# Routed FFN around attention on one core: experts packed eight to a register word, the next tile's rows transposed behind h, and the first steps in another order

## Chip, cores and metric

One Trainium2 chip, one of its cores. The metric is the device time of one execution in microseconds, lower is better. The kernel before took 728.1 us, the median of three runs (727.32 to 729.77).

## What is computed

The input x has 16 x 256 = 4096 rows of 128 numbers (fp32). Three residual stages follow each other:

```python
x = x + 0.5 * ffn(layernorm(x))      # pass 1
x = x + attention(layernorm(x), context)   # 8 heads of 128, 512 keys
x = x + 0.5 * ffn(layernorm(x))      # pass 2, same weights

def ffn(x):      # 8 experts, D 128, F 512; each row goes to the one with the largest logit
    top = argmax(x @ gate_w.T + gate_b + expert_bias)
    for e in range(8):
        h = relu(x @ w1[e] + b1[e])
        out += (top == e) * (h @ w2[e] + b2[e])
```

## The kernel before

**Routing and tiles.** T = 32 tiles of 128 rows. Rows are sorted by expert, so that each tile has one expert, in SLOTS = 39 slots (each expert's region is rounded up to whole tiles: 32 + 8 - 1). In pass 1 VectorE computes for all rows where they go, GpSimd gathers each slot's rows by an indirect DMA (12 buffers), and SyncE stores the results packed. In pass 2 the rows are scattered into sorted regions while attention goes on; SyncE loads the slots, and GpSimd scatters the results to the output. Which expert a slot has is known only on the chip: a table `expert_of_tile` (ET, 39 numbers). In pass 2 it comes in two parts: 17 early slots (EARLY), and 22 late ones, whose table needs the last rows of attention.

**One pass.** Every engine has its own instruction stream, written out as a loop over steps m with lags, and waits for the others by semaphores. In step m TensorE does, in this order (`experts`, L1609):

1. y of tile m-4 (L1649 to L1653): 4 matmuls of 256 columns, 4 of 128, one for the bias; into bank 6 or 7;
2. the transpose of tile m's normed rows (L1659), into bank 0 or 1;
3. h of tile m-1 (L1674, and `three` at L1599 to L1601): 16 matmuls of 128 columns, in fp16 planes (hi by hi, hi by lo, lo by hi).

ScalarE does in step m hT_hi of tile m-2 (L848), xT_hi of tile m (L853) and slot_xn, the normed rows, of tile m+1 (L838). VectorE does the two y additions of tile m-5 (L1330, L1333), hT_lo of tile m-2 (L1338) and xT_lo of tile m (L1342). y waits for hT_lo, for the additions two tiles earlier (its bank) and for the weight planes; h waits for xT_lo, hT_lo four tiles earlier and its planes.

**The expert's registers.** The weights' address depends on the slot's expert. TensorE's stream loads experts into registers with one instruction for up to BATCH = 13 slots (`experts_of`, L387 to L395, the load is L394): ahead of h of slots 0, 13, 17 and 30, in both passes. In pass 2 the one for slot 17 stands behind a wait for the late table. From such a register, register operations make the addresses: the program has groups of three (multiply or add, multiply, add) as one fused operation, and single additions. These, waits and loads are executed by TensorE's sequencer; they aren't counted as busy.

**What else the first steps hold.** Pass 1 begins while other work is still going on, and each engine's stream has a fixed place for it, by step:

```python
W1_PLANES = {0: [3], 1: [4], 2: [5], 3: [6], 4: [7]}           # VectorE: w1_hi, w1_lo of expert e (L1214, L1216)
W2_HIGHS = {1: [2], 3: [3], 4: [4], 5: [5], 6: [6], 7: [7]}    # ScalarE: w2 high plane (L771)
W2_LOWS = {5: [3], 6: [4], 7: [5], 8: [6], 9: [7]}             # VectorE: w2 low plane (L1221)
```

Planes 0 to 2 of w1 are made before step 0 by VectorE, w2's high planes 0 and 1 in step 0 by ScalarE, and w2's low planes 0 to 2 by GpSimd behind its gathers (L617, L621). Tile j of the first eight waits for plane pair j of w1 and w2, whichever expert it has. `head(6)` and `head(7)` are the evacuations on ScalarE (L719, L714) of the last two heads' attention products, which TensorE makes in steps 0 and 1. `packed_rows` (L1108 to L1113) is the table by which SyncE stores packed results, `b2_scale` (L1210) scales a bias that y needs, `scales` (L1233 to L1248) computes the attention's power-of-two scales in step 8, from squares that ScalarE makes in steps 2 and 3 (L736). From step 9 on, ScalarE makes a high plane of the attention matrices every second step (L727, L729; `split_at`), VectorE or GpSimd the low one a step later.

**Around tile 12 of pass 2.** The first 12 slots are loaded ahead. SyncE then fills the tails of the eight regions (`fill_tails`, L402), when the last counts are known in VectorE's step 7, and only then loads slot 12 (L507).

Of the kernel before, what the change touches and what calls it, by code (L numbers as in the profile page):

```python
# [4 lines left out]
P = 128  # L5
# [3 lines left out]
def macaron_kernel(nc, x, context, Wq, Wk, Wv, Wout, bout, gate_w, gate_b, expert_bias, w1, b1, w2, b2, out):  # L9
# [31 lines left out]
    SLOTS = T + E - 1  # L41
# [9 lines left out]
    BATCH = 13  # L51
# [14 lines left out]
    with ctx:  # L66
# [51 lines left out]
        ET = sb("expert_of_tile", [P, SLOTS], i32)  # L118
# [145 lines left out]
        routed = sem("routed")  # L264
# [34 lines left out]
        BATCHES = [*range(0, EARLY, BATCH), *range(EARLY, SLOTS, BATCH)]  # L299
# [15 lines left out]
        SCALES_AT, NORMS = 8, 3 * P  # L315
# [8 lines left out]
        EMPTY_LINKS, EARLY_LINKS = 12, 13  # L324
# [60 lines left out]
        def expert(eng, j):  # L385
            return register_of(eng, ET[0:1, j:j + 1], E - 1)
# [24 lines left out]
        SPLIT_STEP, BIAS_AT = 9, 4  # L411
# [4 lines left out]
        W1_PLANES = {0: [3], 1: [4], 2: [5], 3: [6], 4: [7]}  # L416
        W2_HIGHS = {1: [2], 3: [3], 4: [4], 5: [5], 6: [6], 7: [7]}
# [111 lines left out]
        def _(pool):  # L529
# [25 lines left out]
            def consts_of_second_routing():  # L555
# [3 lines left out]
                          allow_small_or_imprecise_dtypes=True)  # L559
                pool.iota(TIDX[:, :], pattern=[[1, SLOTS]], base=0, channel_multiplier=0,  # L560
# [128 lines left out]
        def _(act):  # L689
# [143 lines left out]
            def experts(r):  # L833
# [8 lines left out]
                def step(m):  # L842
# [36 lines left out]
                if r == 0:  # L879
                    w2_high(0)  # L880
# [53 lines left out]
        def _(dve):  # L934
# [116 lines left out]

            def experts_of_tiles():
                step, count = table_step[0], table_count[0]
# [3 lines left out]
                v.tensor_scalar(ET[:, :], ETF[:, :], float(E - 1), None, ALU.min).then_inc(routed, 1)  # L1057
# [59 lines left out]
            def blocks(first, n, i, after_):  # L1117
                step, count = table_step[1], table_count[1]
                own = slice(first, first + n)
                sel = SEL[:, 0:n, :]  # L1120
# [5 lines left out]
                elif i == 2:  # L1126
                    link(v.tensor_scalar(ET[:, own], ETF[:, 0:n], float(E - 1), None, ALU.min), step, count)
# [138 lines left out]
            pick_rows(1)  # L1266
            split_ranks(0)
# [13 lines left out]
            w1_planes(1)  # L1281
            b1_scale()
            w1_planes(2)
# [39 lines left out]
            def experts(r):  # L1323

                def step(m):
# [27 lines left out]
                    if r == 0 and m == 0:  # L1353
                        packed_rows()
# [183 lines left out]
        def _(pe):  # L1538
# [70 lines left out]
            def experts(r):  # L1609
                loaded = {}  # L1610

                def step(m):
# [17 lines left out]
                    if live(m, 1) and m - 1 in BATCHES:  # L1630
                        some = slice(m - 1, min([b for b in BATCHES if b > m - 1] + [SLOTS]))
                        loaded.update(zip(range(some.start, some.stop), experts_of(pe, some)))
                    if live(m, 4):
# [20 lines left out]
                        last.then_inc(s_y, 1)  # L1654
                    if r == 1 and m > STAT_STEP:
                        last_group(m)
                    if live(m, 0):
                        pe.wait_ge(s_xn, SLOTS * r + m + 1)
                        pe.transpose(BK[m % 2][:, 0:P], XSN[:, m % 2, :], IDN[:, :]).then_inc(s_xT, 1)  # L1659
                    if live(m, 1):  # L1660
                        j = m - 1
                        e1 = loaded[j]
# [296 lines left out]
```

## Time and profile before

| | |
|---|---|
| runs | 727.32, 728.1, 729.77 us |
| profiled execution | 726.75 us, of it 725.0 us from first to last instruction |
| mean granted TensorE clock | 0.979 |
| busy: TensorE, its weight loads | 93%, 63% |
| busy: VectorE, ScalarE, GpSimd | 82%, 80%, 47% |
| pass 1, attention, pass 2 | about 49 to 144, 144 to 614, 614 to 713 us |

The page counts an engine as busy only for its own instructions; TensorE's 93% therefore has in it neither waits nor register work. A matmul's duration in a row is its time through the array, and neighbours overlap: their starts tell the pace. Times in rows are microseconds from the first instruction. "[1.08 <-DVE ...]" is the idle time of the engine just before and what seems to have ended it, "issue" where nothing that the profile shows did. PEld is TensorE's weight load, PEldq its sequencer.

### The profile page before, as it was taken

To read this page: it belongs to the slowest core of one execution; us is meant where nothing else is said; L and a number is where in the kernel's file an instruction comes from. 1 tells how busy PE (TensorE), PEld (TensorE's weight loads), DVE (VectorE), ACT (ScalarE), POOL (GpSimd) and SP (SyncE) were. 2 spreads that over 40 slices of the span, in tenths; PEclk is the share of its full clock that TensorE was granted. 3 is DMA by queue.
4 is the path that set the end of the run, shared out by engine and by line. 5 is a ranking of instruction groups with operands and counts; after the bars stand their busy time and mean duration, and the time that the engine had idled before them with its cause. 6 is when DMAs were issued, how large, how long until landed. Compare 5 with 4: busy or idle time off the path is not lost.

```text
span 725.0 us, 16959 instructions
## 1 busy us (share of the span) xinstructions
PE 675.6 (93%) x5175; PEld 458.5 (63%) x5175; DVE 592.5 (82%) x1598; ACT 578.7 (80%) x1407; POOL 341.0 (47%) x437
## 2 busy tenths in 40 slices
PE   8798888989999999999999999999999999988982
PEld 7677767845666655655655655565565665776872
DVE  6799867887888888888888888888889888676762
ACT  4688666789999999989989989999998997645650
POOL 7056466534434346346445434534634644354433
PEclk9899999999999999999999999999999999999997
DMA  9911333120000000000000000000000020032210
GB/s 244 340 31 33 74 87 82 47 69 2 1 0 1 2 1 16 2 1 11 6 1 9 9 1 5 13 0 1 17 1 2 12 50 0 21 106 54 62 41 5
DMA packets 31029, 26.41 MB, mean 36 GB/s; under 512 B 5001, under 2 KB 26159, under 8 KB 30944
## 3 DMA queue, kind: packets, MB, share of 16 engines
q1 hardware_dynamic: 26496, 18.67, 9.3%
q0 software_dynamic: 3520, 6.40, 3.3%
q8 instruction: 46, 0.75, 0.5%
q10 hardware_dynamic: 928, 0.27, 0.2%
q14 instruction: 39, 0.32, 0.2%
HBM read 15.78 MB, written 10.47 MB: 36 GB/s over the span
## 4 chain that ended last, share of the span: by engine, by line
PE 69%; DVE 14%; ACT 5%; issue 4%; SPq 3%; POOL 2%; DMA 1%; POOLq 0%; DVEq 0%; ACTq 0%
PE bank L1599 14%; PE bank L1601 14%; PE bank L1600 13%; PE bank L1857 13%; PE bank L1649 5%; DVE neg_max L1484 3%; DVE probsT_lo L1490 3%; PE bank L1650 2%; PE bank L1674 2%; DVE hT_lo L1338 2%; ACT probs L894 1%; SPq L448 1%; ACT probsT_hi L901 1%; PE bank L1659 1%; POOL rows L641 1%
## 5 line engine op out<-in xcount | busy, mean ns | idle before, releaser
L657 POOL TENSOR_SCALAR probs<-probs,row_inv 128x512 f32<-128x512 f32 x256 | 177.2, 693 | 250.7 <-DVE row_inv L1495 249.0
L1490 DVE TENSOR_TENSOR probsT_lo<-bank,probsT_hi 128x512 f16<-128x512 f32 x256 | 176.4, 689 | 38.0 <-ACT probsT_hi L901 34.4
L894 ACT ACTIVATE probs<-bank,neg_max_unscaled,unscale_bits 128x512 f32<-128x512 f32 x256 | 199.0, 777 | 8.5
L1484 DVE TENSOR_REDUCE neg_max<-bank 128x1 f32<-128x512 f32 x256 | 175.3, 685 | 24.0 <-PE bank L1601 19.1
L1857 PEld LDWEIGHTS bank<-ident,probs 128*128 128x128 f32 x1024 | 123.8, 141 | 68.5 <-issue 28.8
L1857 PE MATMUL bank<-ident,probs 128*128 128x128 f32 x1024 | 155.0, 274 | 7.4 <-DVE probsT_lo L1490 7.2
L901 ACT ACTIVATE probsT_hi<-bank 128x512 f16<-128x512 f32 x256 | 149.8, 586 | 1.7 <-PE bank L1857 1.7
L889 ACT ACTIVATE neg_max_unscaled<-neg_max,unscale_bits 128x1 f32<-128x1 f32 x256 | 75.1, 293 | 32.2 <-DVE neg_max L1484 27.6
L1599 PE MATMUL bank<-m_hi,xT_hi 128*128 128x512 f16 x256 | 97.0, 379 | 0.8 <-POOL vw_lo L609 0.6
L1601 PE MATMUL bank<-probsT_hi,vw_lo 128*128 128x512 f16 x256 | 97.0, 379 | 0.0
L1599 PE MATMUL bank<-probsT_hi,vw_hi 128*128 128x512 f16 x256 | 97.0, 379 | 0.0
L1600 PE MATMUL bank<-probsT_lo,vw_hi 128*128 128x512 f16 x256 | 97.0, 379 | 0.0
L1601 PE MATMUL bank<-m_hi,xT_lo 128*128 128x512 f16 x256 | 97.0, 379 | 0.0
L1600 PE MATMUL bank<-m_lo,xT_hi 128*128 128x512 f16 x256 | 97.0, 379 | 0.0
L1649 PE MATMUL bank<-w_hi_lo,hT_hi 128*128 x312 | 69.1, 284 | 16.6 <-issue 9.2
L1599 PE MATMUL bank<-slot_xT_hi,w_hi 128*128 128x128 f16 x312 | 70.9, 227 | 0.0
L1674 PE MATMUL bank<-row_picks,bias_planes 128*128 x312 | 69.8, 224 | 0.4 <-DVE slot_xT_lo L1342 0.4
L1600 PE MATMUL bank<-slot_xT_lo,w_hi 128*128 128x128 f16 x312 | 69.9, 224 | 0.0
L1601 PE MATMUL bank<-slot_xT_hi,w_lo 128*128 128x128 f16 x312 | 69.8, 224 | 0.0
L1338 DVE SCALAR_TENSOR_TENSOR hT_lo<-bank,hT_hi 128x512 f16<-128x512 f32 x78 | 53.5, 686 | 19.3 <-ACT hT_hi L848 19.3
L1650 PE MATMUL bank<-w_hi_lo,hT_lo 128*128 x312 | 62.1, 224 | 0.0
L593 POOL DMA_INDIRECT slot_rows<-x_stats,row_of_slot x39 | 41.1, 1053 | 44.4 <-issue 32.5
(261 smaller groups left out, 1172.6 us busy)
## 6 DMA issues: line engine op xcount, KB each, us to landing
w_raw<-in_L_ffn_w SPq DMA_DIRECT2D x16, 256.0 KB, 5.3
x_packed<-slot_rows SPq DMA_DIRECT2D x39, 65.5 KB
slot_rows<-slots SPq DMA_DIRECT2D x39, 65.5 KB, 1.9
x_stats<-rows SPq DMA_DIRECT2D x4, 524.0 KB, 9.9
rows<-x_packed SPq DMA_DIRECT2D x8, 262.0 KB, 3.1
rows<-in_L_attn_x SPq DMA_DIRECT2D x4, 512.0 KB, 8.4
slot_rows<-x_stats,row_of_slot POOLq DMA_INDIRECT x39, 2.9
out<-slot_rows POOLq DMA_INDIRECT x39, 2.6
```

The lines of the kernel that those rows point to most:

```text
L657: pool.tensor_scalar(PR[:, u % 4, :], PR[:, u % 4, :], RI[:, u % 4:u % 4 + 1], 2.0 ** P_BITS, ALU.mult, ALU.mult).then_inc(normed, 1)
L894: act.activation(PR[:, n % 4, :], score_bank(n)[:, :], ACT.Exp, bias=NMS[:, n % 4:n % 4 + 1], scale=MUN, accum_out=SU[:, n % 4:n % 4 + 1]) ...
L901: act.activation(PTH[:, (u // G) % 3, :, (u % G) * P:(u % G + 1) * P], BK[2 + u % 2][:, :].rearrange("p (c q) -> p c q", c=KC), ACT.Copy)\
L1484: v.tensor_reduce(NM[:, n % 4:n % 4 + 1], score_bank(n)[:, :], AX.X, ALU.max, negate=True)\
L1490: v.tensor_tensor(PTL[at], BK[2 + u % 2][:, :].rearrange("p (c q) -> p c q", c=KC), PTH[at], ALU.subtract).then_inc(pT_lo, 1)
L1599: pe.matmul(out_, wh, mh, start=start, stop=False)
L1600: pe.matmul(out_, wh, ml, start=False, stop=False)
L1601: return pe.matmul(out_, wl, mh, start=False, stop=stop)
L1649: pe.matmul(both, HTH[:, j % 3, own], W2HL[:, ds(e, 1), c, :, :], start=(c == 0), stop=False)
L1650: last = pe.matmul(y_, HTL[:, j % 3, own], W2HL[:, ds(e, 1), c, 0, :], start=False, stop=(c == FC - 1))
L1674: pe.matmul(h_, BIAS[:, own], PICK[:, ds(e1, 1), :], start=True, stop=False)
L1857: last = pe.transpose(BK[2 + u % 2][:, c * P:(c + 1) * P], PR[:, u % 4, c * P:(c + 1) * P], IDN[:, :])
```

## The change

**Packing.** The table of experts isn't stored as 39 integers but as words, eight experts of three bits in one: VectorE multiplies each slot's expert by a power of two (`shifted`) and adds eight neighbours (`into_words`). Pass 1 has five words, loaded at once in step 1; pass 2 has three for the early slots, loaded in step 1, and three for the late ones, loaded in step 18. For each tile TensorE's sequencer shifts the word and masks it, behind y and before the transpose and h (`expert_in`). The powers are made once: an iota and a memset on GpSimd among its constants, a shift on VectorE behind the second `pick_rows`.

**Transpose.** From tile 14 of pass 1 and tile 10 of pass 2 on, the transpose of tile m+1 stands behind h of tile m-1, at the end of step m, instead of that of tile m between y and h.

**First steps of pass 1.** w1's planes 1 to 7 are made one per step, in steps 0 to 6; ScalarE makes w2's high plane e in step e; `head(7)` moves on ScalarE from step 1 to step 2; `y_unscale` and `b2_scale` move from step 1 to 3, `packed_rows` from 0 to 4, the squares from 2 and 3 to 7 and 8, `scales` from 8 to 10, and the high planes of attention start in step 11 instead of 9 and are spread to end in the same step 39.

```diff
-    BATCH = 13
+    WORD_TILES, EXPERT_BITS = 8, 3
...
+        EARLY_WORDS = -(-EARLY // WORD_TILES)
...
-        SCALES_AT, NORMS = 8, 3 * P
+        SCALES_AT, NORMS = 10, 3 * P
...
-        def experts_of(eng, tiles_):
+        def word_of(r, j):
+
+            if r == 0 or j < EARLY:
+                return divmod(j, WORD_TILES)
+            word, place = divmod(j - EARLY, WORD_TILES)
+            return EARLY_WORDS + word, place
+
+        def load_words(eng, words):
 
             regs = []
-            for j in range(tiles_.start, tiles_.stop):
+            for _ in range(words.start, words.stop):
                 registers[0] += 1
                 regs.append(eng.alloc_register(f"loaded{registers[0]}"))
-            eng.reg_load(regs, ET[0:1, tiles_])
-            return [eng.snap(reg, donate=True, min_val=0, max_val=E - 1) for reg in regs]
+            eng.reg_load(regs, WORDS[0:1, words])
+            return dict(zip(range(words.start, words.stop), regs))
+
+        def expert_in(eng, word, place):
+
+            registers[0] += 1
+            reg = eng.alloc_register(f"loaded{registers[0]}")
+            eng.reg_alu(reg, word, EXPERT_BITS * place, ALU.logical_shift_right)
+            eng.reg_alu(reg, reg, E - 1, ALU.bitwise_and)
+            return eng.snap(reg, donate=True, min_val=0, max_val=E - 1)
...
-        SPLIT_STEP, BIAS_AT = 9, 4
+        SPLIT_STEP, BIAS_AT = 11, 4
+        ROWS_AHEAD = (14, 10)
...
-        W1_PLANES = {0: [3], 1: [4], 2: [5], 3: [6], 4: [7]}
-        W2_HIGHS = {1: [2], 3: [3], 4: [4], 5: [5], 6: [6], 7: [7]}
+        W1_PLANES = {e - 1: [e] for e in range(1, E)}
+        W2_HIGHS = {e: [e] for e in range(E)}
...
         def split_at(m, lag):
-            k, odd = divmod(m - lag - SPLIT_STEP, 2)
-            return [divmod(k, 2)] if not odd and 0 <= k < 2 * H else []
+            return [divmod(k, 2) for k in range(2 * H) if m - lag - SPLIT_STEP == 15 * k // 8]
...
+                pool.memset(SHIFTED[:, :, :], 0.0)
+                pool.iota(POWER[:, :, :], pattern=[[0, 6], [EXPERT_BITS, WORD_TILES]], base=127, channel_multiplier=0)
...
-                    if r == 0 and m == 0:
-                        w2_high(1)
...
-                    if r == 0 and m < 2:
-                        head(BEFORE_FFN + m)
-                    if r == 0 and m in (2, 3):
-                        ww_square(m - 2)
+                    if r == 0 and m in (0, 2):
+                        head(BEFORE_FFN + m // 2)
+                    if r == 0 and m in (SCALES_AT - 3, SCALES_AT - 2):
+                        ww_square(m - SCALES_AT + 3)
...
                 slot_norm(0)
-                if r == 0:
-                    w2_high(0)
...
+            def powers():
+
+                dve.wait_ge(consts_ready, 4)
+                v.tensor_scalar(POWER[:, :, :], POWER[:, :, :], 23, None, ALU.logical_shift_left).then_inc(powers_ready, 1)
+
+            def shifted(first, n):
+
+                return v.scalar_tensor_tensor(out=SHIFTED[:, :, :].rearrange("p w t -> p (w t)")[:, first:first + n],
+                                              in0=ETF[:, 0:n], scalar=float(E - 1),
+                                              in1=POWER[:, :, :].rearrange("p w t -> p (w t)")[:, first:first + n].bitcast(fp32),
+                                              op0=ALU.min, op1=ALU.mult)
+
+            def into_words(first, n):
+
+                with nc.allow_low_precision(reason="whole numbers below 2 ** 24 are exact"):
+                    return v.tensor_reduce(WORDS[:, first:first + n], SHIFTED[:, first:first + n, :], AX.X, ALU.add)
...
-                v.tensor_scalar(ET[:, :], ETF[:, :], float(E - 1), None, ALU.min).then_inc(routed, 1)
+                link(shifted(0, SLOTS), step, count)
+                into_words(0, -(-SLOTS // WORD_TILES)).then_inc(routed, 1)
...
             w1_planes(0)
             bias_rest(2)
-            w1_planes(1)
             b1_scale()
-            w1_planes(2)
...
-                    if r == 0 and m == 1:
+                    if r == 0 and m == 3:
                         y_unscale()
                         b2_scale()
...
-                    if r == 0 and m == 0:
+                    if r == 0 and m == 4:
                         packed_rows()
...
+                def rows_transposed(m):
+                    pe.wait_ge(s_xn, SLOTS * r + m + 1)
+                    pe.transpose(BK[m % 2][:, 0:P], XSN[:, m % 2, :], IDN[:, :]).then_inc(s_xT, 1)
...
-                    if live(m, 1) and m - 1 in BATCHES:
-                        some = slice(m - 1, min([b for b in BATCHES if b > m - 1] + [SLOTS]))
-                        loaded.update(zip(range(some.start, some.stop), experts_of(pe, some)))
+                    if m == 1:
+                        words.update(load_words(pe, slice(0, EARLY_WORDS if r else -(-SLOTS // WORD_TILES))))
+                    if r == 1 and m == EARLY + 1:
+                        words.update(load_words(pe, slice(EARLY_WORDS, 6)))
...
                         last.then_inc(s_y, 1)
+                    if live(m, 1):
+                        word, place = word_of(r, m - 1)
+                        e1 = loaded[m - 1] = expert_in(pe, words[word], place)
                     if r == 1 and m > STAT_STEP:
                         last_group(m)
-                    if live(m, 0):
-                        pe.wait_ge(s_xn, SLOTS * r + m + 1)
-                        pe.transpose(BK[m % 2][:, 0:P], XSN[:, m % 2, :], IDN[:, :]).then_inc(s_xT, 1)
+                    if live(m, 0) and m < ROWS_AHEAD[r]:
+                        rows_transposed(m)
...
                         last.then_inc(s_h, 1)
+                    if live(m + 1, 0) and m + 1 >= ROWS_AHEAD[r]:
+                        rows_transposed(m + 1)
```

## Rows read from the trace of the kernel before

**Rows 1.** The page: busy us (share of the span) xinstructions of each engine.
```profile
PE 675.6 (93%) x5175; PEld 458.5 (63%) x5175; DVE 592.5 (82%) x1598; ACT 578.7 (80%) x1407; POOL 341.0 (47%) x437
```

**Rows 2.** Windows by stage: us, each engine's busy us (xinstructions), granted clock, DMA.
```profile
64.00:84.00 20.00, 16.91 (x226) 14.34 (x224) 19.24 (x54) 13.90 (x33) 8.04 (x9) 1.00 0.20 46
96.00:121.00 25.00, 24.84 (x328) 21.27 (x329) 19.68 (x51) 18.15 (x43) 15.92 (x17) 1.00 0.34 78
124.00:128.00 4.00, 4.00 (x34) 3.55 (x35) 1.29 (x4) 1.86 (x4) 2.06 (x3) 0.60 0.32 88
128.00:134.00 6.00, 6.00 (x89) 5.59 (x86) 5.41 (x21) 4.48 (x11) 4.57 (x5) 0.98 0.14 39
```

**Rows 3.** Sequencer's work (PEldq) by line, 96 to 121 us: ns min/median/max, first and last start.
```profile
L1644 PEldq EVENT_SEMAPHORE  x12: 51/51/51, 97.7 to 119.6; - x12
...
L1649 PEldq FUSED_REGOPS  x51: 46/46/46, 96.1 to 120.2; - x51
```

**Rows 4.** Timeline of weight loads, one steady tile: start us, us, line, [idle before].
```profile
105.47 0.10 PEld L1600 LDWEIGHTS bank<-slot_xT_lo,w_hi 128*128 x1
105.55 0.10 PEld L1601 LDWEIGHTS bank<-slot_xT_hi,w_lo 128*128 x1
105.83 0.10 PEld L1649 LDWEIGHTS bank<-w_hi_lo,hT_hi 128*128 128x128 f16 x1 [0.19 <-issue]
```

**Rows 5.** Register loads of TensorE (L394): in 90 to 100, in 615 to 652 us.
```profile
L394 PEldq TENSOR_LOAD <-expert_of_tile x1: 3130/3130/3130, 92.6 to 92.6; - x1
...
L394 PEldq TENSOR_LOAD <-expert_of_tile x2: 1007/1057/1107, 618.7 to 649.8; - x2
```

**Rows 6.** TensorE's timeline: the first y matmul behind each of five loads.
```profile
84.67 0.28 PE L1649 MATMUL bank<-w_hi_lo,hT_hi 128*128 x1 [1.08 <-DVE slot_rows L1333]
...
95.96 0.28 PE L1649 MATMUL bank<-w_hi_lo,hT_hi 128*128 x1 [3.28 <-issue]
...
124.00 0.28 PE L1649 MATMUL bank<-w_hi_lo,hT_hi 128*128 x1 [2.25 <-DVE hT_lo L1338]
...
662.31 0.28 PE L1649 MATMUL bank<-w_hi_lo,hT_hi 128*128 x1 [3.29 <-issue]
...
690.74 0.28 PE L1649 MATMUL bank<-w_hi_lo,hT_hi 128*128 x1 [2.44 <-issue]
```

**Rows 7.** TensorE's timeline around tile 12 of pass 2.
```profile
643.16 0.28 PE L1649 MATMUL bank<-w_hi_lo,hT_hi 128*128 x1
...
646.64 0.33 PE L1659 MATMUL bank<-ident,slot_xn 128*128 128x128 f32 x1 [2.57 <-ACT slot_xn L838]
```

**Rows 8.** SyncE's timeline: the fills ahead of tile 12's load.
```profile
635.15 6.57 SPq L402 DMA_DIRECT2D slots<-fill  x8
```

**Rows 9.** VectorE's timeline, first steps of pass 1.
```profile
49.36 0.35 DVE L1207 TENSOR_SCALAR bias_planes<-bias_planes,h_scale 128x512 bf16<-128x512 bf16 x1
...
51.24 0.47 DVE L1214 TENSOR_SCALAR w_hi<-w_raw,w_then_w_scale_bits 128x512 f16<-128x512 f32 x1
...
52.42 0.48 DVE L1108 TENSOR_TENSOR sel<-sel,counts 128x312 f32<-128x312 f32 x1
...
55.44 0.69 DVE L1210 TENSOR_SCALAR bias_planes<-bias_planes,h_scale,w_then_w_scale_bits 128x128 bf16<-128x128 bf16 x1
...
58.56 1.57 DVE L1216 SCALAR_TENSOR_TENSOR w_lo<-w_raw,w_then_w_scale_bits,w_hi 128x512 f16<-128x512 f32 x1
```

**Rows 10.** ScalarE's timeline, the same steps.
```profile
48.59 0.73 ACT L767 ACTIVATE bias_planes<-b_b_rows 32x640 bf16<-32x640 f32 x1
...
52.78 0.27 ACT L853 ACTIVATE slot_xT_hi<-bank 128x128 f16<-128x128 f32 x1
```

**Rows 11.** TensorE's timeline: y of tile 0, the transpose of tile 13.
```profile
59.65 0.28 PE L1649 MATMUL bank<-w_hi_lo,hT_hi 128*128 x1
...
82.41 0.28 PE L1659 MATMUL bank<-ident,slot_xn 128*128 128x128 f32 x1
```

**Rows 12.** GpSimd's timeline: the w2 plane beside VectorE's w1_lo.
```profile
58.43 1.16 POOL L621 TENSOR_TENSOR w_hi_lo<-w_raw,w_hi_lo 128x512 f16<-128x512 f32 x1 [0.18 <-POOL w_raw L617]
```

More of the change, by code:

```diff
@@ L117, in macaron_kernel @@
         TAIL = sb("region_tail", [P, E], i32)
-        ET = sb("expert_of_tile", [P, SLOTS], i32)
+        POWER = sb("power_of_tile", [P, 6, WORD_TILES], i32)
+        SHIFTED = sb("shifted_expert", [P, 6, WORD_TILES], fp32)
+        WORDS = sb("experts_of_tiles", [P, 6], i32)
         TB = sb("block_of_tile", [P, SLOTS], i32)
@@ L263, in macaron_kernel @@
         table_step = [sem(f"table_step{r}") for r in range(2)]
-        routed = sem("routed")
+        routed, powers_ready = sem("routed"), sem("powers_ready")
         tail_ready, tail_filled = sem("tail_ready"), sem("tail_filled")
@@ L298, in macaron_kernel @@
         LATE = SLOTS - EARLY
-        BATCHES = [*range(0, EARLY, BATCH), *range(EARLY, SLOTS, BATCH)]
+        EARLY_WORDS = -(-EARLY // WORD_TILES)
         W1_SUMS, W1_SQUARES = E + 1, E + 1
@@ L312, in macaron_kernel @@
         ROW_STEP, STAT_STEP, LOGIT_STEP, RANK_STEP = 1, 2, 4, 7
-        SCALES_AT, NORMS = 8, 3 * P
+        SCALES_AT, NORMS = 10, 3 * P
         LEAST_EXP = 77
         M_QUARTERS, V_QUARTERS = 4 * 1 - 14 + 1, 1
-        EMPTY_LINKS, EARLY_LINKS = 12, 13
+        EMPTY_LINKS, EARLY_LINKS = 13, 14
         def router_bank(g, step=0):
@@ L1050, in ends_of @@
                      table_step[r], table_count[r])
+            def powers():
[9 more added lines that the diff above has]
+                    return v.tensor_reduce(WORDS[:, first:first + n], SHIFTED[:, first:first + n, :], AX.X, ALU.add)
             def experts_of_tiles():
+                dve.wait_ge(powers_ready, 1)
                 step, count = table_step[0], table_count[0]
@@ L1119, in blocks @@
                 own = slice(first, first + n)
+                first_word = EARLY_WORDS if first else 0
                 sel = SEL[:, 0:n, :]
@@ L1126, in blocks @@
                 elif i == 2:
-                    link(v.tensor_scalar(ET[:, own], ETF[:, 0:n], float(E - 1), None, ALU.min), step, count)
+                    link(shifted(first_word * WORD_TILES, n), step, count)
+                    link(into_words(first_word, -(-n // WORD_TILES)), step, count)
                 elif i == 3:
@@ L1266, in _ @@
             pick_rows(1)
+            powers()
             split_ranks(0)
@@ L1609, in experts @@
             def experts(r):
-                loaded = {}
+                words, loaded = {}, {}
+                def rows_transposed(m):
+                    pe.wait_ge(s_xn, SLOTS * r + m + 1)
+                    pe.transpose(BK[m % 2][:, 0:P], XSN[:, m % 2, :], IDN[:, :]).then_inc(s_xT, 1)
                 def step(m):
@@ L1654, in step @@
                         last.then_inc(s_y, 1)
+                    if live(m, 1):
+                        word, place = word_of(r, m - 1)
+                        e1 = loaded[m - 1] = expert_in(pe, words[word], place)
                     if r == 1 and m > STAT_STEP:
                         last_group(m)
-                    if live(m, 0):
-                        pe.wait_ge(s_xn, SLOTS * r + m + 1)
-                        pe.transpose(BK[m % 2][:, 0:P], XSN[:, m % 2, :], IDN[:, :]).then_inc(s_xT, 1)
+                    if live(m, 0) and m < ROWS_AHEAD[r]:
+                        rows_transposed(m)
                     if live(m, 1):
                         j = m - 1
-                        e1 = loaded[j]
                         if r == 0 and j == 0:
```

2 lines of the change are left out of this document (removed).

## The prediction

> **What bounds the kernel now.** The page first: TensorE is busy for 675.6 of 725.0 us [rows 1], so what counts is where it pauses or is slowed in the two FFN passes; the attention between them, 144 to 614 us, isn't touched. Then the windows by stage [rows 2]. From 64 to 84 us VectorE is busy for 19.24 of 20 us and TensorE for 16.91: the first tiles are bound by VectorE, which beside its own work per tile makes the weight planes, the tables and the scales. From 96 to 121 us TensorE is busy for 24.84 of 25 us with 328 matmuls, 26 for a tile, so 1.98 us a tile. But it isn't its array that sets this pace. At 128 to 134 us, just after a stretch at a low clock in which its sequencer could get ahead, 89 matmuls go into 6.0 us, 1.75 us a tile. I read the sequencer next [rows 3, 4]. In a steady tile it executes, beside 26 weight loads and 26 matmuls, two waits (L1644, L1670), nine fused register operations (L1649 four, L1599 four, L1674 one) and five single ones (L1601 four, L1653 one); two of these lines stand in the group, with 12 and 51 executions in some 12.6 tiles. What one of them costs is seen in the starts of the weight loads [rows 4]: L1600 to L1601, with a single register operation between, is 0.08 us (105.47 to 105.55), and L1601 to the next tile's L1649, with a wait and a fused one between, 0.28 (to 105.83), reported as 0.19 idle behind "issue". So a wait or a fused operation costs about 0.1 us and a single one 0.06. Two, nine and five of them are 1.4 us, and the instructions between them fill most of the rest of 1.98: in the steady stretches the sequencer is the bound, and has no lead.
>
> Last the register loads. A load of 13 experts takes 3.13 us, 0.24 per register; the two in the row of 1007/1057/1107 ns are hidden, one by four queued attention slots, one by a stretch at the low clock [rows 5]. Behind the five loads that aren't hidden the first y matmul comes after pauses of 1.08, 3.28, 2.25, 3.29 and 2.44 us [rows 6].
>
> **Loads.** One load of five words at the head of pass 1 and one of three at the head of pass 2 lie where 13-register loads lie hidden now: nothing. Of the five pauses 0.17 each is the usual gap at this place: 12.34 - 0.85 = 11.5 us go. Pass 2 keeps one load, of three words, in step 18, behind the same wait for the late table: 3 x 0.24 = 0.7 (below: 0.3, by the cheap 13 in 1107 ns; above 1.0, what four registers cost). Net -10.8.
>
> **Clock.** Two of these pauses are followed by a stretch with a granted clock near 0.6, so mostly at 1.2 GHz instead of 2.4: at 124 to 128 us 34 matmuls instead of 52 (13.1 per us) run, 18 too few; by 134 us ten are made up [rows 2]. That is 0.6 us, and the same behind the pause at 690 a little less. With the pauses gone: -1.0 (bounds 0 and -2; a pause that stays may fall so too).
>
> **The register operations.** Per tile a shift and an AND are added, between y and h. Nothing in the trace shows them. They depend on nothing but a register loaded long before, and as neighbours I expect them as one fused operation: 0.10 us. Lower bound 0, if some lead hides them; upper 0.21, two at the price of a wait. In the tiles that are bound by VectorE it is hidden; 24 tiles of pass 1 and 23 of pass 2 behind its long wait carry it, with some 3 of the earlier tiles: 50 x 0.10 = +5.0 (0 to +10.5). The Trainium skill (Advanced Engine Details and Errata, Sequencer Loop and Engine Queue Depths) says that other instructions can be queued while a control instruction runs, and gives TensorE a queue of 64. By that alone these operations would be free, with a median of 719.8 us.
>
> **The transpose behind h.** The matmuls and waits are the same, in another order: the transpose's own wait rides on its weight load. While the sequencer is the bound it matters little whether the array has 0.12 us of work behind y or behind h: 0 (from -0.11 a tile, if it fills most of the 0.17 pause before y, to 0). Its inputs are in time: ScalarE is busy for 18.15 of 25 us in the steady window [rows 2] and makes slot_xn a step ahead. At one place it costs. Tile 12 of pass 2 waits 2.57 us for its rows [rows 7], whose load SyncE can issue only behind eight fills, 635.15 plus 6.57 us [rows 8]. Now y of tile 8, some 0.75 us from 643.16 on, is done before that wait; in the new order tile 12's transpose stands ahead of it and y comes behind. +0.8.
>
> **The first steps.** VectorE is nearly always busy until 84 us [rows 2], so every pause put in shifts the steps, until TensorE binds. I walked the new order with today's durations. A plane pair is 1.2 us (51.24 to 52.42) [rows 9]. (1) Between the last bias rest and the bias scaling at 49.36, which waits for ScalarE's bias plane (48.59 + 0.73) [rows 10], a plane pair is made now; in the new order 1.2 us are idle. (2) Tile 0's xT_hi comes hardly earlier than now, while its xT_lo is next on VectorE: 0.7. (3) In step 0 ScalarE has head 6 and then one w2 plane, 0.6 us, ahead of tile 1's xT_hi, now at 52.78 with both w2 planes in the shade of waits for TensorE: 53.4. VectorE has tile 0's xT_lo done at 50.7 and plane 1 at 51.9, and waits 1.6. (4) In step 2 head 7 (two evacuations of 0.5) and a w2 plane now stand ahead of tile 1's hT_hi, done near 58.1, when plane 3 is done at 57.1: 1.0. Together 4.5. Moving planes, packed_rows (some 2 us from 52.42) and scales from one VectorE step to another adds nothing to their sum. It makes y of tile 0 wait for the b2 scaling, which ends near 60.2 (now 55.44 + 0.69), with that y at 59.65 now [rows 11]: within the 4.5. Two things take some back. The w1_lo at 58.56 takes 1.57 us, where the pair above leaves 1.2 - 0.47 for one, while GpSimd's L621 runs from 58.43 on [rows 12]; in the new order VectorE is idle or at short work there: -0.8. And VectorE has 0.76 us without work in the window to 84 us, where TensorE binds already, and will have none: some -1.0. That leaves +2.7 (bounds +1 and +4.5). The Trainium skill (SBUF — State Buffer, two separate sides) has VectorE and GpSimd share a port pair as an exclusive lock, so whichever starts second waits for a whole instruction; the stretch in the trace agrees, and by this rule a plane of the new order could meet it as well, which would give 725.6 us.
>
> **Tables.** One operation becomes two or three small ones: +0.2 us before the first planes, which then ends in pause (1); powers() falls into VectorE's wait for the first ranks; GpSimd's two constants are as small as its iotas, and the rstd behind them waits for VectorE. packed_rows four steps later holds SyncE's first store, which needs y(0) anyway. +0. ScalarE's squares at steps 7 and 8 are ahead of the scales at step 10; the head planes end in the same step 39. 0.
>
> **Sum.** -10.8 - 1.0 + 5.0 + 0.8 + 2.7 = -3.3 us. The profiled execution took 726.75 us (span 725.0), 1.35 under the median of 728.1; it would come to 723.4, and the median to 724.8.
>
> **Rivals.** A, the sequencer keeps a lead: for it, a load of 1.1 us vanishes behind four slots, and 1.75 us a tile occurs; against it, 0.19 us "issue" before nearly every y. The register operations are then free and the transpose fills 0.11 of each pause: -3.3 - 5.0 - 5.2 = -13.5, 714.6 us; with the first alone 719.8. B, the other side, slower: the extraction costs the sequencer two full operations plus a late restart of h, 0.22 us a tile and more; it decides from 0.21 on (0.10 + 5.5 / 50). At 0.22: 50 x 0.12 = +6.0 on the sum, 730.8 us. For it, a fused operation is never under 0.1 us and the two might not fuse; against it, single ones cost 0.06. C, no difference: the removed pauses are paid back in the first steps, where VectorE gets 4.5 us of pauses and nothing is recovered, and the clock falls elsewhere: +1.8 and +1.0, 727.6. That the packing doesn't take effect can't be: five loads of 13 or so are gone from the program.
>
> **Numbers.** Forecast 0.48, A in part or whole 0.19, C 0.19, B 0.14. Range from 717.0 (between A's two values) to 730.0 (short of B). 0.3% is 2.2 us, about what a measurement of this kernel tells from no change. Faster by more: most of the forecast, A: 0.60. Within: the rest of it and C: 0.27. Slower: B, 0.13.
>
> **What would show it.** Right: no pause over 1 us at the old load places but one of about 0.9 in step 18; one more fused operation per tile; a steady tile at 2.08 us, 312 matmuls in 25 us instead of 328; the transpose of tile 13 near 85 us (now 82.41 [rows 11]); y of tile 8 behind the transpose of tile 12. Wrong: a steady tile at 1.9 us or less, or 2.2; VectorE without pauses before 60 us; attention starting later than 144 us.

## The result, and the profile after

The changed kernel took 730.93 us, the median of 17 runs (729.25 to 735.0), beside 728.07 us for the kernel before on the same chips. The ratio is 1.0031, 95% interval 1.0018 to 1.0044. The difference of the medians is 2.9 us (by the interval 1.3 to 3.2), slower, where 724.8 was forecast, with a range that ended at 730.0. "Ratio" below is always to the kernel before, timed beside on the same chip; a difference in us is that of the medians.

The page of the changed kernel begins so (its profiled execution):

```profile
span 729.7 us, 17116 instructions
...
PE 687.3 (94%) x5175; PEld 457.0 (63%) x5175; DVE 591.8 (81%) x1602; ACT 575.4 (79%) x1407; POOL 342.6 (47%) x439
```

TensorE has the same 5175 matmuls as in [rows 1] and is "busy" for 11.7 us longer. They have not become longer: the durations of all of them together are 1497.5 us before and 1496.2 after. Each is reported with 0.22 to 0.28 us and overlaps its neighbours, so matmuls that start further apart still cover the time between them, and count as busy for more of it. The windows by stage, with the columns of [rows 2]:

```profile
64.00:84.00 20.00, 16.97 (x193) 13.48 (x192) 19.34 (x52) 13.43 (x30) 7.61 (x7) 0.94 0.18 42
96.00:121.00 25.00, 24.05 (x296) 18.79 (x294) 19.11 (x51) 16.41 (x39) 15.04 (x15) 1.00 0.33 76
665.00:690.00 25.00, 24.19 (x293) 18.91 (x294) 16.40 (x44) 12.29 (x33) 10.75 (x11) 1.00 0.22 56
```

In the steady stretch of 96 to 121 us 296 matmuls run in 25 us instead of 328: 26 x 25 / 296 = 2.20 us a tile instead of 1.98, where 2.08 was forecast. What was forecast for the loads came: the three loads of words take 0.78 us each, and one pause stays at an old load place, behind the load in step 18 of pass 2. The first row has all three loads, the second that one, the third is the first y behind it:

```profile
L400 PEldq TENSOR_LOAD <-experts_of_tiles x3: 781/783/792, 51.4 to 664.0; - x3
...
L400 PEldq TENSOR_LOAD <-experts_of_tiles x1: 792/792/792, 664.0 to 664.0; - x1
...
665.01 0.28 PE L1686 MATMUL bank<-w_hi_lo,hT_hi 128*128 x1 [0.74 <-issue]
```

VectorE's first steps show the four pauses that the forecast had walked through (1.2, 0.7, 1.6, 1.0 us), the last one smaller:

```profile
50.50 0.35 DVE L1240 TENSOR_SCALAR bias_planes<-bias_planes,h_scale 128x512 bf16<-128x512 bf16 x1 [1.45 <-ACT bias_planes L783]
51.71 0.29 DVE L1374 SCALAR_TENSOR_TENSOR slot_xT_lo<-bank,slot_xT_hi 128x128 f16<-128x128 f32 x1 [0.86 <-ACT slot_xT_hi L869]
...
54.83 0.29 DVE L1374 SCALAR_TENSOR_TENSOR slot_xT_lo<-bank,slot_xT_hi 128x128 f16<-128x128 f32 x1 [1.65 <-ACT slot_xT_hi L869]
...
59.28 0.69 DVE L1370 SCALAR_TENSOR_TENSOR hT_lo<-bank,hT_hi 128x512 f16<-128x512 f32 x1 [0.27 <-ACT hT_hi L864]
...
63.76 1.56 DVE L1249 SCALAR_TENSOR_TENSOR w_lo<-w_raw,w_then_w_scale_bits,w_hi 128x512 f16<-128x512 f32 x1
```

The w1_lo of 1.56 us again runs beside a w2 plane of GpSimd, as the one of 1.57 did in [rows 9, 12]:

```profile
63.62 1.15 POOL L637 TENSOR_TENSOR w_hi_lo<-w_raw,w_hi_lo 128x512 f16<-128x512 f32 x1 [0.18 <-POOL w_raw L633]
```

### The profile page after: what moved, and what is told of

It is laid out like the page before. It is cut to its first block, busy times and chain, and to the rows that moved or that the text cites. A ratio compares the mean times of both kernels' runs of the same rounds, so it can differ in the third digit from the quotient of the medians.

```text
span 729.7 us, 17116 instructions
## 1 busy us (share of the span) xinstructions
PE 687.3 (94%) x5175; PEld 457.0 (63%) x5175; DVE 591.8 (81%) x1602; ACT 575.4 (79%) x1407; POOL 342.6 (47%) x439
## 4 chain that ended last, share of the span: by engine, by line
PE 69%; DVE 13%; ACT 4%; issue 4%; SPq 3%; DMA 3%; POOL 2%; POOLq 0%; DVEq 0%
PE bank L1631 14%; PE bank L1633 13%; PE bank L1632 13%; PE bank L1897 13%; PE bank L1686 4%; DVE neg_max L1516 3%; PE bank L1712 3%; DVE probsT_lo L1522 3%; DMA x_packed<-slot_rows 2%; PE bank L1687 2%; ACT probs L906 1%; SPq L462 1%; ACT probsT_hi L913 1%; PE bank L1646 1%; POOL rows L657 1%
## 5 line engine op out<-in xcount | busy, mean ns | idle before, releaser
L864 ACT ACTIVATE hT_hi<-bank 128x512 f16<-128x512 f32 x78 | 46.4, 595 | 54.0 <-PE bank L1633 54.0
L1686 PE MATMUL bank<-w_hi_lo,hT_hi 128*128 x312 | 67.4, 280 | 7.0 <-DVE slot_rows L1365 3.9
```

Source lines behind the costliest of these rows:

```text
L1686: pe.matmul(both, HTH[:, j % 3, own], W2HL[:, ds(e, 1), c, :, :], start=(c == 0), stop=False)
```

## What a register operation costs

The page doesn't count the sequencer's own instructions, but the trace has their starts. The next table isn't a view of the profile: it is worked out from those starts, for the steady stretch of 96 to 121 us, as the median time from the start of one instruction of TensorE's sequencer to the start of the next (us). The last three rows are of the kernel with the packing alone (below).

```
kernel before:  fused (L1599, L1649, L1674) -> next             0.124
                single (L1601, L1653)       -> next             0.113
                wait (L1644, L1670)         -> next             0.106
packing alone:  fused L1693  -> shift L407                      0.124
                shift L407   -> AND L408                        0.154   (0.127 to 0.251)
                AND L408     -> wait ahead of h L1715           0.117
```

A single register operation costs nearly what a fused one costs, not the half of it. Between most of these pairs matmuls are issued. Where nothing stands between, from the AND to the next wait in the changed kernel, it is 0.097. Nine fused, five single and two waits make 9 x 0.124 + 5 x 0.113 + 2 x 0.106 = 1.89 us of the tile's 1.98, so the sequencer's bound could have been summed from the trace of before, and two more single operations at 0.113 make 0.23. In the changed kernel they stand as two operations, 0.14 to 0.25 us apart, in every tile:

```profile
L407 PEldq ALU_OP  x11: 36/36/36, 97.2 to 119.5; - x11
...
L408 PEldq ALU_OP  x11: 36/36/36, 97.4 to 119.7; - x11
```

Their duration of 36 ns says nothing of this price: what counts is the time until the next one starts.

## Experiments: each part alone

Four kernels were timed together, with the kernel before at 728.45 us (35 executions).

**The packing alone** (steps and transpose as before):

```diff
-        ROWS_AHEAD = (14, 10)
+        ROWS_AHEAD = (SLOTS + 9, SLOTS + 9)
...
-        W1_PLANES = {e - 1: [e] for e in range(1, E)}
+        W1_PLANES = {0: [3], 1: [4], 2: [5], 3: [6], 4: [7]}
```

(and every other step's place likewise)

> The packing alone, with the steps and the place of the transpose as before. Theory P (the shift and the AND cost TensorE's sequencer 0.23 us a tile, as two operations, which the changed kernel's trace suggests, and carried by about 50 tiles): -10.8 for the loads, -1.0 for the clock, +11.7, so 728.0 us, within 1.5 of the kernel before, and a steady tile of 2.21 to 2.25 us. Rival S (the pair costs about 0.1 as forecast, and the loss is in the first steps or in the transpose behind h): -6.8, some 721.3 us, a steady tile of 2.08.

Measured: 727.1 us, ratio 0.998 (0.9952 to 1.0008), -1.35 us. The steady stretch, pass 1 and then pass 2:

```profile
96.00:121.00 25.00, 24.96 (x296) 19.41 (x293) 19.80 (x50) 16.78 (x40) 15.27 (x17) 1.00 0.32 76
...
690.00:710.00 20.00, 19.22 (x235) 15.37 (x234) 14.05 (x35) 10.22 (x24) 8.80 (x10) 1.00 0.12 36
```

296 matmuls in 25 us, with neither steps nor transpose changed. So the slower tile is the packing's own, and takes back all but 1.35 us of what the loads had given (the interval of that rest is -3.5 to +0.6 us). Theory P held within its margin.

**The first steps alone:**

```diff
-        W1_PLANES = {0: [3], 1: [4], 2: [5], 3: [6], 4: [7]}
-        W2_HIGHS = {1: [2], 3: [3], 4: [4], 5: [5], 6: [6], 7: [7]}
+        W1_PLANES = {e - 1: [e] for e in range(1, E)}
+        W2_HIGHS = {e: [e] for e in range(E)}
...
             bias_rest(2)
-            w1_planes(1)
             b1_scale()
-            w1_planes(2)
```

> The first steps' order alone. Theory P: +2.7 as forecast, 730.8 us, with the transpose of tile 13 near 85.2 us instead of 82.4 and VectorE with three pauses of about 1 us before 60 us. Rival S: +7 or more, over 735 us. Rival Z (the pauses are made up later): within 1 us of the kernel before.

Measured: 731.08 us, 1.0046 (1.0023 to 1.0069), +2.6 us. VectorE's pauses are 1.44, 0.86, 1.64 and 0.27 us, and from the transpose of tile 0 to that of tile 13 it takes 35.2 us instead of 32.5.

**The transpose behind h alone:**

```diff
-                    if live(m, 0):
-                        pe.wait_ge(s_xn, SLOTS * r + m + 1)
-                        pe.transpose(...)
+                    if live(m, 0) and m < ROWS_AHEAD[r]:
+                        rows_transposed(m)
...
                         last.then_inc(s_h, 1)
+                    if live(m + 1, 0) and m + 1 >= ROWS_AHEAD[r]:
+                        rows_transposed(m + 1)
```

> The transpose behind h alone, with the old register loads. Theory P: +0.8 us, from y of tile 8 behind the late rows of tile 12 in pass 2, and a steady tile of 1.98 us as before. Rival S: a steady tile of 2.05 or more (h restarts late or xT comes late), +3 us or more. Rival G: it fills part of the 0.17 us before y, a steady tile of 1.9, -3 us or more.

Measured: 730.21 us, 1.0025 (1.0002 to 1.0047), +1.8 us (0.1 to 3.4), so the forecast's 0.8 lies in the interval. Its steady tiles take 1.9 to 2.1 us from transpose to transpose, as those of the kernel before do: nothing per tile, neither S nor G. But the same stretch in the windows is different from [rows 2]:

```profile
96.00:121.00 25.00, 24.09 (x291) 21.13 (x292) 16.92 (x44) 14.91 (x36) 16.00 (x17) 0.87 0.36 86
```

The granted clock is 0.87 where it was 1.00. Behind the load of 13 registers TensorE runs at the lower clock (1.2 GHz) for 6.8 us; two windows of four show it:

```profile
95.00:99.00 4.00, 2.12 (x17) 1.88 (x18) 1.17 (x4) 0.00 (x0) 2.13 (x2) 0.61 0.50 134
99.00:103.00 4.00, 4.00 (x37) 3.69 (x36) 1.81 (x5) 1.76 (x4) 0.69 (x1) 0.54 0.21 54
```

**All but the packing:** both edits above, with the register loads as before.

> The changed kernel without the packing: the steps and the transpose as changed, the register loads as before. Theory P: 728.1 + 2.7 + 0.8 = 731.6 us, about the changed kernel's time, since the packing gives nothing. Rival S: 735 us or more. If the parts don't add up (interaction), it differs from the sum of the steps alone and the transpose alone by over 1.5 us.

Measured: 733.93 us, 1.0075 (1.0052 to 1.0098), +5.5 us, where the two parts alone sum to 4.4; within the intervals that is additive, and it lies between theory P's 731.6 and rival S's 735. Put on this kernel the packing gives 2.6 us (from +5.5 to +2.9 over the kernel before, each beside its own), on the kernel before 1.35. So it is no loss by itself; but by the forecast's terms it was to give 6.8 and pay for the other two parts, and it doesn't.

## Experiments: where the transpose costs, and the sequencer's price again

**The changed kernel with the transpose in its old place** (`ROWS_AHEAD` past the last step, packing and steps as changed), beside the kernel before at 727.85 us:

> The changed kernel with the transpose back between y and h in every step (packing and first steps as changed). If the parts add up (packing alone -1.35, steps alone +2.6), +1.3 us on the kernel before, and the transpose behind h costs the changed kernel 1.6 us. Rival: behind h it costs only where long register loads make TensorE pause and its clock fall; the packed kernel has none, so it costs 0.8 us or less here (y of tile 8 behind the late tile 12), and this kernel stands +2.1 us or more over the kernel before.

Measured: 729.82 us, 1.0009 (0.9988 to 1.0031), +2.0 us. This doesn't decide between the two: the interval is -0.9 to +2.3 us and holds both +1.3 and +2.1. By the medians the transpose behind h costs the changed kernel 0.9 us, by the ratios (1.0031 against 1.0009) 1.6. In the profiled executions pass 1 is 0.7 us longer with it and pass 2 1.0: from tile 12's transpose to the last y of pass 2 the changed kernel takes 66.2 us, this one 65.2. The changed kernel's rows show where: y of tile 8 (and in pass 1, at one place, y of tile 28) now starts behind a transpose that waits for its rows.

```profile
650.60 0.48 PE L1646 MATMUL bank<-ident,slot_xn 128*128 128x128 f32 x1 [2.46 <-ACT slot_xn L854]
650.87 0.42 PE L1686 MATMUL bank<-w_hi_lo,hT_hi 128*128 x1
...
128.63 0.33 PE L1646 MATMUL bank<-ident,slot_xn 128*128 128x128 f32 x1 [0.73 <-ACT slot_xn L854]
128.83 0.28 PE L1686 MATMUL bank<-w_hi_lo,hT_hi 128*128 x1
```

**The transpose alone, in pass 2 from tile 13 on** (`ROWS_AHEAD = (14, 13)` on the kernel before):

> The transpose alone behind h, but in pass 2 from tile 13 instead of tile 10 on, so that tile 12's, with its late rows, stays behind y of tile 8. If the forecast's term is right, 0.8 us less than the transpose alone from 10 (+1.8 us on the kernel before), so +1.0 us. If the stretches at the low clock make the +1.8, +1.8 us again, with three such stretches in a pass instead of two.

Measured: 730.19 us, 1.0022 (0.9987 to 1.0057), +2.3 us. The interval, -0.9 to +4.1 us, holds both expectations, so the medians don't decide. The traces have more stretches at the low clock in the three kernels with this transpose and long loads (table below), but the profiled execution of one kernel is one of many. The record has the mean granted clock of every execution beside its time, so executions can be compared at equal clock (medians in us; how many in brackets):

```
                            granted clock     with it        kernel before
transpose alone             0.975 to 0.976    731.7 (5)      729.2 (10; 0.974 to 0.976)
                            0.979 to 0.981    729.7 (5)      728.0 (6)
transpose, from 13          0.974 to 0.976    729.1 (5)      728.9 (6)
                            0.978 to 0.980    728.9 (2)      727.9 (3)
```

(The last line leaves out two executions of each kernel that took over 735 us.)

At equal clock the transpose alone is still 2.5 and 1.7 us slower, and its median clock, 0.978, is nearly that of the kernel before, 0.979: the low clock doesn't explain its +1.8. With the transpose of pass 2 from tile 13 on, 0.2 and 1.0 us are left at equal clock, and the median clock is lower, 0.976 beside 0.982. That fits the forecast's reading, y of tile 8 behind the late tile 12, better than the rival with the clock. It is a comparison of few executions, made afterwards, and what of the +1.8 is tile 12's isn't shown.

The next two ran on another chip, on which the kernel before took 751.93 us (in the traces from there the eight fills take 10.2 to 10.9 us, where the others have 6.5 to 7.3); they are compared there.

**The pair made twice:**

```diff
             eng.reg_alu(reg, word, EXPERT_BITS * place, ALU.logical_shift_right)
             eng.reg_alu(reg, reg, E - 1, ALU.bitwise_and)
+            eng.reg_alu(reg, word, EXPERT_BITS * place, ALU.logical_shift_right)
+            eng.reg_alu(reg, reg, E - 1, ALU.bitwise_and)
```

> The packing alone with the shift and the AND made twice per tile (the second pair repeats the first into the same register). Theory P: each operation of such a chain takes TensorE's sequencer about 0.12 us and nothing hides it in the steady tiles, so a steady tile goes from 2.22 to 2.45 us and the time from 727.1 to 727.1 + 50 x 0.23 = 738.6 us. Rival S (only the restart of h behind the pair costs, a fixed amount per tile): 2.22 and about 727 us.

Measured: 754.32 us, 1.0035 (1.0006 to 1.0064). The edit did less than it says: the trace has L407, L409 and L410 in each tile and no L408, so the first AND, whose result nothing read, isn't in the program. One operation was added, not two, and the forecast of 738.6 us, for two, can't be held against it. A window to put beside the packing alone's x235, and two of the three operations:

```profile
690.00:710.00 20.00, 19.97 (x226) 15.02 (x223) 13.61 (x35) 10.63 (x25) 8.25 (x10) 1.00 0.21 55
...
L409 PEldq ALU_OP  x11: 32/33/33, 686.5 to 709.5; - x11
...
L410 PEldq ALU_OP  x11: 36/36/36, 686.6 to 709.6; - x11
```

A tile goes from 2.21 (26 x 20 / 235) to 2.30 us: 0.09 for one more operation. Rival S, a fixed amount for the restart of h, would have left 2.21. Over tiles 20 to 29 of pass 2, from transpose to transpose, it is 2.23 and 2.31 us.

**The pair apart** (the shift ahead of y's waits, the AND left where it was):

> The packing alone with the shift ahead of y (behind the load, before y's waits) and the AND where it was, so that the AND never waits for a shift just made. Theory P1 (each operation costs its own 0.1 to 0.12 us wherever it stands): no change from the packing alone, 727 us, a steady tile of 2.22. Theory P2 (most of it is the AND waiting for the shift's result): single operations cost 0.06 as forecast, 0.12 for both, a steady tile of 2.10 and 727.1 - 50 x 0.11 = 721.6 us.

Measured: 752.58 us, 1.002 (0.9987 to 1.0052), and the same tile:

```profile
690.00:710.00 20.00, 18.56 (x237) 15.50 (x236) 13.35 (x37) 11.29 (x27) 8.64 (x10) 1.00 0.20 56
```

26 x 20 / 237 = 2.19 us, and 2.23 from transpose to transpose. P1 holds for the tile: the pair costs the same wherever the shift stands, and the AND's waiting for the shift is no part of it. This rests on the tile, not on the times: the packing alone wasn't run on this chip, and these two kernels' medians differ by 1.7 us, where 50 x 0.08 makes 4. Their pass 1 has many tiles of 3 us and more there, in which an operation can be hidden, and takes 114.3 and 114.1 us; pass 2 takes 103.0 and 101.7.

## Experiments: why some loads were quick

One thing in [rows 5] hadn't been asked: 13 registers take 1.1 us in one load and 3.1 in another. The forecast used the 1.1 only as a lower bound. But the quick loads all begin at slot 0, and the slow ones at slots 13, 17 and 30, which are 52, 68 and 120 bytes into the table.

```diff
-        ET = sb("expert_of_tile", [P, SLOTS], i32)
+        ET = sb("expert_of_tile", [P, 4, 16], i32)
...
-            eng.reg_load(regs, ET[0:1, tiles_])
+            eng.reg_load(regs, ET[0:1, table_row(r, tiles_.start), 0:tiles_.stop - tiles_.start])
```

(each batch has a row of 16 words, 64 bytes, of its own, written by one VectorE operation more per table in pass 2; nothing is packed. Pass 1 also has three batches of 13 now instead of 13, 4, 13 and 9, so one load fewer.)

> The kernel before with the table of experts laid out so that each batch of the register load starts at a 64-byte boundary in SBUF (pass 1 in three batches of 13 instead of 13, 4, 13, 9). Theory A (a load of registers is quick, 1.1 us for 13, only where its words start aligned as those of slot 0 do, and takes 0.24 us per register elsewhere): all loads of 13 take 1.1 to 1.3 us, the pauses fall from 11.5 us to about 5, and the time from 728.1 to about 721 us. Rival H (the first load of a pass is quick because of what goes on beside it, not because of its address): the loads at slots 13 and later still take 3.1 us, 728 us or one or two more.

Measured: 746.97 us where the kernel before took 751.93, 0.9921 (0.9889 to 0.9953). On a chip like the first (before: 727.85):

> The aligned loads again, the same kernel, beside the kernel before. Loads of 13 in 1.1 us: -5 us and more on the kernel before (-0.8% there), four stretches at low clock or fewer in the two passes. If the gain came only from that chip, less than 2 us.

Measured: 721.28 us, 0.9907 (0.9876 to 0.9938), -6.6 us. In its trace four of the pauses behind loads are left, of 1.31, 1.33, 1.17 and 0.97 us, 4.8 together instead of 12.3. Its loads, all seven, then those at slots 26 (pass 1), 17 and 30 (pass 2), and the pause behind the last:

```profile
L398 PEldq TENSOR_LOAD <-expert_of_tile x7: 340/1105/1297, 51.2 to 683.9; - x7
...
L398 PEldq TENSOR_LOAD <-expert_of_tile x1: 1231/1231/1231, 111.6 to 111.6; - x1
...
L398 PEldq TENSOR_LOAD <-expert_of_tile x1: 1105/1105/1105, 656.7 to 656.7; - x1
...
L398 PEldq TENSOR_LOAD <-expert_of_tile x1: 839/839/839, 683.9 to 683.9; - x1
...
685.03 0.28 PE L1656 MATMUL bank<-w_hi_lo,hT_hi 128*128 x1 [0.97 <-DVE slot_rows L1340]
```

Loads of 13, 9 and 4 registers in the midst of a pass take 1.1 to 1.25, 0.84 and 0.34 us instead of 3.1 to 3.2, 2.2 to 2.3 and 1.0. Theory A holds for the loads; how much of the 6.6 us is the one load fewer wasn't separated (the pause behind the load of 4 registers in pass 1 was 1.08 us [rows 6]). An estimate from these times: 0.1 us, and 0.25 for each full group of four registers and for each one left over (3 + 1 for 13, 2 + 1 for 9, 1 for 4); from the other starts 0.24 for each register. The changed kernel's loads of three words, one of them from the table's start, take 0.78 us, like three single ones; its load of five, with a wait in it, takes the same. Whether a start at 16 bytes suffices, or it has to be 32 or 64, wasn't tried.

**And the loads in hidden places:**

```diff
+        LOADS_AHEAD = ({1: [0], 5: [1], 9: [2]}, {1: [0, 1]})      # step: batches
+        LATE_AT = 12
...
+                    if r == 1 and m == LATE_AT:
+                        pe.wait_ge(routed, 3)
+                        load_batches([2, 3])
                     if live(m, 0):
```

> As the aligned one, and the loads moved to where TensorE waits anyway: in pass 1 ahead of y in steps 1, 5 and 9, where VectorE is the bound, in pass 2 the 17 early slots in step 1 and the 22 late ones in step 12, ahead of the wait for tile 12's rows. Theory A: all five pauses go and nothing is paid for them, with up to four stretches of low clock fewer: 728.1 - 11.5 - 1 to 2.5 = 714 to 715.6 us. Rival H (13 registers take 3.1 us wherever they stand): step 5 pays 2.5, step 9 1.5 and step 12 of pass 2 3 us of it again, 722 to 724 us.

> The aligned loads in hidden places again, the same kernel. On the chip of the first run, gathered rows came late in pass 1 (waits of 2.5 us for slots' rows) and took back what the loads had given. Where they come in time: -11.5 - 1 to 2.5 us, 714 to 715.6 us if the kernel before takes 728.1. If its moved loads cost elsewhere, no better than the aligned one beside it.

Measured: 747.9 us (0.9966, 0.9937 to 0.9996) on the slower chip, and 720.55 us (0.9887, 0.9848 to 0.9926) on the other, -7.3 us: 0.7 us better than the aligned one here and 0.9 worse on the slower chip, where 6 or more were expected. The expectation that nothing is paid for them wasn't met. The pauses at the loads are gone, and from the first transpose of a pass to its last y it takes 94.0 and 87.0 us, against 95.6 and 88.5: 3.1 us, not the 4.8 of the pauses. In the profiled execution 2.7 us of these go again ahead of pass 1, whose first transpose starts at 53.5 us instead of 50.8; whether that is this kernel's or chance isn't shown. What is late next is the gathered rows: in pass 1 TensorE waits 4.4 us in four places for ScalarE's normed rows (3.7 in the aligned one). The waits of TensorE from 51 to 150 us, first row, and one of the four:

```profile
PE bank L1673 <- ACT slot_xn L844: 4.4, 4, 1.6
...
126.44 0.33 PE L1673 MATMUL bank<-ident,slot_xn 128*128 128x128 f32 x1 [1.56 <-ACT slot_xn L844]
```

All kernels of the first kind of chip side by side, worked out from their traces: the median less that of the kernel before beside it; from the first transpose of a pass to the start of its last y matmul of hT_hi; and the stretches at the lower clock (1.2 GHz) in the two passes, from windows of 0.5 us (each was 3.4 us long; those of 6.8 us count twice).

```
                        median    pass 1   pass 2   low stretches
kernel before             0        97.6     93.7        4
changed kernel          +2.9      100.4     94.6        2
packing alone           -1.35      96.9     93.2        0
first steps alone       +2.6      100.4     93.5        3
transpose alone         +1.8       99.6     95.8        6
all but the packing     +5.5      100.5     95.8        5
changed, old transpose  +2.0       99.7     93.6        1
transpose, from 13      +2.3       98.7     95.5        7
loads aligned           -6.6       95.6     88.5        1
aligned and hidden      -7.3       94.0     87.0        3
```

## Why the prediction was wrong, point by point

- **The register operations** are the step that failed: "a wait or a fused operation costs about 0.1 us and a single one 0.06", and "as neighbours I expect them as one fused operation: 0.10 us". They weren't fused, and a single one costs 0.11. The 0.06 came from the starts of two weight loads [rows 4]. Those rows show when the array took the weights, behind what was queued; the price of the sequencer is in its own starts. With the tile at 2.20 us instead of 1.98 the term is 50 x 0.22 = 11 us, just over its upper bound of 10.5 and not at the +5.0 that was taken. What showed it: the starts above, the packing alone (2.21 us a tile with nothing else changed), and one more operation, which makes it 2.30. Put into the sum, -3.3 becomes +2.7 and the forecast 730.8; measured were 730.9. That it meets to 0.1 us is luck: 50 tiles was an estimate, and the other terms are known to a microsecond at best (below). Rival B had the price (0.22) and the time (730.8), and the chance of 0.14 was far too small; its second half, a late restart of h, wasn't needed.
- **Loads:** -10.8 was right as far as the rows tell: all pauses went but one, of 0.74 where 0.9 was forecast. **Clock:** -1.0 stood for two low stretches, and in the packing alone all four of the two passes went. By these terms it gives -10.8 - 1.0 + 11 = -0.8 us; measured were -1.35, no difference within the interval. The kernel before has the price of the clock in its own executions: ten with 0.974 to 0.976 took 729.2 us, eight with 0.983 took 727.5, 1.7 us for some 3.5 stretches of 3.4 us fewer. So -1.0 for two was about right, and all four would be near -2.
- **The first steps:** +2.7 forecast, +2.6 measured, but partly by luck. Pause 4 was 0.27 and not 1.0, the others were longer than walked through, 4.2 us together instead of 4.5; and the 0.8 us for the long w1_lo never came back, because a w1_lo of the new order ran beside GpSimd's plane as well (1.56 us). With these two, the sum would be 4.2 - 1.0 = +3.2; the interval of the measurement, 1.7 to 5.0 us, holds both. By the rule of the Trainium skill (SBUF — State Buffer, two separate sides), an exclusive lock on the port pair that VectorE and GpSimd share, the new order could meet this too; the trace agrees, with the rows of 1.56 and 1.15 us above.
- **The transpose:** 0 per tile held, and y of tile 8 behind tile 12 is there as forecast, at 1.0 us for 0.8 (66.2 against 65.2). Pass 1, for which nothing was forecast, is 0.7 us longer in the profiled execution, with tile 28's y behind a wait of 0.73. As a whole the edit costs 0.9 to 1.6 us in the changed kernel and 1.8 alone, with 0.8 inside both intervals; so the term may be too small, and the record doesn't settle it.
- **Rival A** fell: in the steady tiles there is no lead. The operations lengthened the steady tile by their own price, 0.22 us for two and 0.08 to 0.09 for one more, so nothing of them was hidden there. The Trainium skill (Advanced Engine Details and Errata, Sequencer Loop) says that other instructions can be read and queued while a control instruction runs. By that alone it would be 719.8 us, against 730.9 measured.
- **The range** ended at 730.0, just "short of B", because B was held unlikely.

## What to carry to other kernels

Where TensorE's stream holds many register operations, sum the sequencer first: starts of its own instructions, from one to the next, in one steady tile. If that sum is near the tile's time, an operation per tile is paid in full, and trading a load of 0.24 us per register for two operations of 0.11 each is no trade; what the packing gave, 1.35 us, isn't clear of zero. Before packing a table, look at why the load is slow; here a layout that starts each batch at a multiple of 64 bytes in the table (and has one load fewer) gave 6.6 us with no operation added per tile.

## What wasn't expected of the hardware

- A load of 13 registers takes 1.1 to 1.25 us from a row of its own in the table (a start at a multiple of 64 bytes) and 3.1 from a start at 68 bytes, and 9 take 0.84 against 2.2 to 2.3.
- A single register operation takes TensorE's sequencer 0.113 us from start to next start, a fused one of three 0.124.
- The head of the program isn't steady: the first transpose of pass 1 starts between 49.9 and 53.5 us, once at 56.9, in profiles of kernels that differ little or nothing ahead of it; the one at 56.9 took 735.6 us, 5.8 over its kernel's median. Two profiles' spans can't be compared to a microsecond. Stretches within a pass are free of that, but not of how many stretches at the low clock this execution had: the transpose alone has 4.1 us more in its two passes, and 1.8 in the medians.
- One chip took 3% longer for the same kernels. Its attention was as long as on the others (471 us from the last y of pass 1 to the first transpose of pass 2), but from the transpose of tile 9 to that of tile 10 in pass 2 it took 8.8 to 9.2 us instead of 2.
